# Last normalisation for all tokens beside the last expert unit, and that unit's own rows patched in behind it

## The chip, the cores and the metric

The kernel runs on one core of one Trainium2 chip. The metric is the device time of one execution in microseconds (us), the median of several. TensorE (PE) multiplies matrices, VectorE (DVE) and ScalarE (ACT) work elementwise, GpSimd (POOL) does small elementwise work and issues the indirect and the accumulating DMAs, SyncE (SP) issues plain DMAs.

## What is computed

The input is 8 x 512 = 4096 tokens of 256 floats. The first half of the reference (two attentions and a normalisation with a residual) isn't touched by the change. The second half is a mixture of experts with its own normalisation and residual:

```
logits = xf @ w_router;  probs = softmax(logits)
topk_w, topk_idx = top_k(probs, 2)            # each token: 2 of 8 experts
h   = gelu(einsum('te,ieh->tih', xf, w1) + b1)      # 256 -> 1024
out = einsum('tih,ihe->tie', h, w2) + b2            # 1024 -> 256
out = sum(out * weights, axis=1)
x = x + layernorm(ffn(layernorm(x)))
```

So a token's output row is its kept row x plus the normalised sum of two expert rows. A normalisation needs both.

## The kernel before

Stage 1 computes x (kept in the SBUF tile `X`, 32 rows of 256 in each of 128 partitions) and scatters every token's row twice into the HBM tensor `expert_rows`, sorted by expert. Tables made on VectorE (`fill_tables`) cut these rows into 39 subtiles of 256.

Stage 2 (`stage2`) runs 23 units over them: units 0 to 15 are pairs (two subtiles, 4 blocks of 128 rows), units 16 to 22 are singles (2 blocks). Unit t does this:

- SP loads the expert's weights into `WG1` and `WG2`; POOL gathers the unit's rows into `XG` (`gather_rows`, L1514), one indirect DMA for each block, two units ahead.
- TensorE turns the rows (`turn`, L1772), multiplies by the first weights into `PH` (`first`, L1761) and by the second ones into `PY` and `PB` (`second`, L1792 and L1793). ScalarE applies gelu (L1603) and makes the high parts of weights and hidden values, VectorE the low parts (L1691, L1696, L1702).
- VectorE computes the unit's gates `G` (`note`, L1681), POOL the weighted bias `BW` (`weigh_bias`, L1539), VectorE the result rows `Y` (`result`, L1659 and L1662), in the first groups of the next unit.
- POOL scatters `Y` with an add into the HBM tensor `choice_rows` (`send`, L1528), one indirect DMA for each block. `send(t)` waits until those of unit t-1 have landed, since both may hit the same row.

Every engine's order is fixed by the loops over t, over the groups j of the first product and over the eight chunks c of the second one: POOL gathers for t+2 and sends t-1 in the last group of t, and weighs the bias of t+1 at c = 6. Semaphores do the rest. While units 5 to 9 run, SP writes the kept rows of five of the eight batches to the output tensor `out` (L1492).

Stage 3 (`stage3`) starts when all of `choice_rows` has landed. SP loads it batch by batch (512 rows, `YC`, L1861). For each batch VectorE makes mean and variance (L1900 to L1906), POOL the inverse root (L1875, L1877), ScalarE the normalised rows `T` (L1914). The first five batches are then added by POOL to the kept rows in `out` with an accumulating DMA (L1881); for the last three VectorE adds `X` (L1894) and SP stores the sum (L1865).

## Time and profile before

| | us |
|---|---|
| median of 3 runs (1081.58 to 1086.25) | 1084.42 |
| the profiled execution, its own time | 1075.38 |
| its span, first to last instruction | 1073.6 |
| last matmul of the last unit starts | 1036.81 |
| first load of stage 3 is issued | 1043.30 |
| PE busy / DVE / ACT / POOL | 974.2 / 676.9 / 730.8 / 403.8 |
| mean granted TensorE clock | 0.968 |

The busy times are averages over stages with different limits. What is late at the end is read from the last 60 us, in which TensorE first works at nearly 100% and then not at all.

### The profile page before, as it was taken

To read this page: it belongs to the slowest core of one execution; us is meant where nothing else is said; L and a number is where in the kernel's file an instruction comes from. 1 tells how busy PE (TensorE), PEld (TensorE's weight loads), DVE (VectorE), ACT (ScalarE), POOL (GpSimd) and SP (SyncE) were. 2 spreads that over 40 slices of the span, in tenths; PEclk is the share of its full clock that TensorE was granted. 3 is DMA by queue.
4 is the path that set the end of the run, shared out by engine and by line. 5 is a ranking of instruction groups with operands and counts; after the bars stand their busy time and mean duration, and the time that the engine had idled before them with its cause. 6 is when DMAs were issued, how large, how long until landed. Compare 5 with 4: busy or idle time off the path is not lost.

```text
span 1073.6 us, 16809 instructions
## 1 busy us (share of the span) xinstructions
PE 974.2 (91%) x5468; PEld 659.2 (61%) x5468; DVE 676.9 (63%) x1882; ACT 730.8 (68%) x1124; POOL 403.8 (38%) x348
## 2 busy tenths in 40 slices
PE   5799999999999999978889988999999999998960
PEld 3233545455454545434588877888888888888850
DVE  5235286564838654554785789567766776777857
ACT  3688777777867777756737554676666677666836
POOL 4101020413223050304334357655555545545436
PEclk9899999999999999989999999999999999999995
DMA  7664726437181684822413443856655545567839
GB/s 277 140 231 85 263 46 213 126 102 251 39 270 56 227 300 114 320 82 90 158 61 104 104 128 69 262 154 152 157 158 135 171 128 119 123 166 215 235 56 287
DMA packets 57695, 171.12 MB, mean 159 GB/s; under 512 B 10384, under 2 KB 26896, under 8 KB 51728
## 3 DMA queue, kind: packets, MB, share of 16 engines
q1 hardware_dynamic: 38698, 137.99, 38.7%
q0 software_dynamic: 18768, 31.76, 15.5%
q8 instruction: 39, 0.64, 0.3%
q10 hardware_dynamic: 150, 0.41, 0.2%
q14 instruction: 40, 0.33, 0.1%
HBM read 98.55 MB, written 71.57 MB: 158 GB/s over the span
## 4 chain that ended last, share of the span: by engine, by line
PE 69%; DVE 13%; ACT 6%; issue 5%; DMA 3%; POOL 3%; ACTq 0%; SPq 0%; DVEq 0%; POOLq 0%
PE PH L1761 15%; PE PO L979 8%; PE PS L996 8%; PE PB L1059 7%; PE PY L1792 5%; PE PB L1792 4%; ACT E L603 3%; PE PY L1797 3%; PE PA L1046 3%; PE PY L1793 3%; PE PA L1027 3%; PE PB L1793 2%; DVE HP L1702 2%; PE PA L1036 1%; PE PT L1772 1%
## 5 line engine op out<-in xcount | busy, mean ns | idle before, releaser
L603 ACT ACTIVATE E<-PS,VV 128x1024 f32<-128x1024 f32 x256 | 271.2, 1118 | 66.9 <-PE PS L996 66.7
L1761 PE MATMUL PH<-XP,W1P 128*128 128x512 f32 (+1 forms) x1104 | 231.3, 367 | 13.5 <-DVE HP L1702 9.0
L1761 PEld LDWEIGHTS PH<-XP,W1P 128*128 128x128 f32 x1104 | 184.3, 191 | 54.7 <-DVE HP L1702 12.7
L1528 POOL DMA_INDIRECT choice_rows<-Y,DI x78 | 130.5, 1673 | 119.4 <-DVE Y L1662 96.8
L996 PE MATMUL PS<-OPB,OPA 102*128 102x512 bf16 x512 | 140.1, 388 | 13.4 <-ACT E L603 7.2
L1702 DVE TENSOR_TENSOR HP<-PH,HP 128x512 fp32r<-128x512 f32 x156 | 106.8, 686 | 65.5 <-ACT HP L1608 65.2
L979 PE MATMUL PO<-E,VA 128*32 128x512 f32 x1024 | 144.9, 616 | 0.0
L1603 ACT ACTIVATE PH<-PH,B 128x512 f32<-128x512 f32 (+1 forms) x184 | 107.5, 596 | 52.3 <-PE PH L1761 43.1
L996 PEld LDWEIGHTS PS<-OPB,OPA 102*128 102x128 bf16 x512 | 36.9, 98 | 160.1 <-ACT E L603 81.5
L1594 ACT CAST W2P<-WG 128x512 fp32r<-128x512 f32 x92 | 56.7, 621 | 102.2 <-PE PB L1793 63.2
L469 POOL DMA_INDIRECT expert_rows<-PAY,SLOT x64 | 63.0, 985 | 155.9 <-issue 81.9
L1792 PE MATMUL PY<-W2P,HP 128*128 128x512 f32 x288 | 108.5, 407 | 2.2 <-DVE Y L1662 2.2
L1696 DVE TENSOR_TENSOR W2P<-WG,W2P 128x512 fp32r<-128x512 f32 x92 | 74.6, 818 | 55.3 <-ACT W2P L1594 54.0
L1608 ACT CAST HP<-PH 128x512 fp32r<-128x512 f32 x156 | 91.6, 587 | 4.9
L1514 POOL DMA_INDIRECT XG<-expert_rows,RI x78 | 81.9, 1050 | 26.7 <-issue 22.7
L1793 PE MATMUL PY<-W2P,HP 128*128 128x256 f32 x288 | 80.5, 279 | 0.0
L1792 PE MATMUL PB<-W2P,HP 128*128 128x512 f32 x176 | 65.4, 395 | 0.0
L1691 DVE TENSOR_TENSOR W1P<-WG,W1P 128x512 fp32r<-128x512 f32 x92 | 59.7, 687 | 8.4 <-ACT W1P L1587 8.3
L1792 PEld LDWEIGHTS PY<-W2P,HP 128*128 128x128 f32 x288 | 54.1, 188 | 15.2 <-DVE Y L1662 3.8
L1797 PE MATMUL PY<-W2P,HP 128*128 128x256 f32 x480 | 63.1, 289 | 0.0
L1539 POOL TENSOR_TENSOR BW<-WG,G 128x1024 f32<-128x1024 f32 (+1 forms) x23 | 41.7, 1813 | 54.0 <-DVE G L1681 54.0
L491 POOL TENSOR_TENSOR SM<-SM,HALF 128x4 f32<-128x4 f32 x16 | 18.4, 1150 | 113.3 <-DVE SM L206 113.3
(244 smaller groups left out, 1559.4 us busy)
## 6 DMA issues: line engine op xcount, KB each, us to landing
expert_rows<-ZERO SPq DMA_DIRECT2D x8, 4160.0 KB, 12.9
WG<-experts SPq DMA_DIRECT2D x23, 1152.0 KB, 5.8
WG<-experts SPq DMA_DIRECT2D x23, 1028.0 KB, 5.2
OPB<-q_parts SPq DMA_DIRECT2D x192, 64.0 KB
q_parts<-QP SPq DMA_DIRECT2D x48, 128.0 KB
OPA<-q_parts SPq DMA_DIRECT2D x31, 192.0 KB
choice_rows<-ZERO SPq DMA_DIRECT2D x1, 5120.0 KB, 14.4
X<-x SPq DMA_DIRECT2D x8, 512.0 KB, 8.0
```

What stands on the lines that cost most here:

```text
L603: a.activation(E[:, s % 2, h, :, :], PS[:, u % 2, :, :], ACT.Exp, scale=vec("tau_t")[:, 4 * (s // 2) + h:4 * (s // 2) + h + 1]).then_inc(e ...
L979: i = t.matmul(PO[32 * h:32 * h + 32, :], VA[:, par, 2 * jp + jc, 4 * g + h, :], E[:, s % 2, h, jc, :], start=(jp == 0 and jc == 0), stop= ...
L996: ins = t.matmul(PS[:, u % 2, jc, :], OPA[0:KA, m, key:key + P], OPB[0:KA, m, hh * N:hh * N + N], start=True, stop=True)
L1514: g.indirect_dma_start(out=XG[:, t % 2, i, :], out_offset=None, in_=rows, in_offset=IND(ap=RI[:, b // HALVES, b % HALVES:b % HALVES + 1], ...
L1528: g.indirect_dma_start(out=ys, out_offset=IND(ap=DI[:, t % 3, i:i + 1], axis=0), in_=Y[:, t % 2, i, :], in_offset=None, compute_op=ALU.add ...
L1603: last = a.activation(r, r, ACT.Gelu_apprx_tanh, bias=B1[:, n * j + k:n * j + k + 1])
L1608: a.copy(region(0, j), PH[:, u % BANKS, :]).then_inc(h_hi, 1)
L1702: v.tensor_tensor(region(1, j), PH[:, u % BANKS, :], region(0, j).bitcast(f32), ALU.subtract).then_inc(h_lo, 1)
L1761: last = m.matmul(PH[:, u % BANKS, at:at + w], W1P[:, a, k * HID + c * P:k * HID + c * P + P], XP[:, o, k, 0:w], start=(k == 0 and (a, o) ...
L1792: m.matmul(sums(i), HP[:, 0, at:at + P], W2P[:, c, :, :], start=(c == 0), stop=(c == HC - 1), skip_group_check=True)
L1793: last = m.matmul(sums(i)[:, 0, :], HP[:, 1, at:at + P], W2P[:, c, 0, :], start=False, stop=(c == HC - 1), skip_group_check=True)
L1797: last = m.matmul(PY[:, i, :], HP[:, a, at:at + P], W2P[:, c, o, :], start=(c == 0 and (a, o) == terms[0] and i % 2 == 0), stop=(c == HC - ...
```

## The change

It moves three things.

1. One pair is put behind the singles: units 0 to 14 are pairs, 15 to 21 singles, and unit 22, the last, is a pair. Tables keep their layout (`entry_of`, `subtile_of`).
2. Stage 3 for all tokens runs beside unit 22. It waits for the sends of units 20 and 21 only, loads `choice_rows` into `X`, normalises in place and adds all eight batches into `out` with accumulating DMAs. So that `X` is free, SP writes all eight batches of kept rows beforehand, each twice: to `out` and to a new HBM tensor `kept_rows`. For the rows of unit 22 what it writes isn't final.
3. Unit 22 isn't sent to `choice_rows`. POOL gathers, by the token numbers `TO` of its 4 x 128 rows, their kept rows (`gather_kept`) and what the other units have summed for them (`gather_partial`). VectorE adds the latter to `BW`, so that `result` gives whole rows in `Y`; these are normalised like a batch, their kept rows added, and POOL scatters them over `out` (plain writes, `out_patched`), each of the four scatters waiting until the one before has landed, the first until all eight adds have.

One small comparison (`HOLDS`) is new in the tables: it sets the gates of unit 22 to zero if the unit holds no rows.

```diff
-KEPT = 5
...
+    xs = nc.dram_tensor("kept_rows", (TOK, D), f32, kind="Internal").ap()
...
+def is_pair(t):
+
+    return t < PAIRS - 1 or t == NUNITS - 1
+
+
+def entry_of(t):
+
+    return t if t < PAIRS - 1 else PAIRS - 1 if t == NUNITS - 1 else t + 1
...
-    return 2 * HALVES if t < PAIRS else HALVES
+    return 2 * HALVES if is_pair(t) else HALVES
...
-    return HID // P if t < PAIRS else HID // P // 2
+    return HID // P if is_pair(t) else HID // P // 2
...
-    return first_block(t) // HALVES
+    e = entry_of(t)
+    return 2 * e if e < PAIRS else PAIRS + e
...
+    link(v.tensor_tensor(HOLDS[:, :], first[:, 2 * LEFT_PAIRS - 2:2 * LEFT_PAIRS - 1], limit[:, 2 * LEFT_PAIRS - 2:2 * LEFT_PAIRS - 1], ALU.is_lt))
...
+    TBL = blocks_of(LAST)
+    kept, partial = (WG1[:, k * TB * D:(k + 1) * TB * D].rearrange("p (i e) -> p i e", e=D) for k in range(2))
...
+    PARTIAL = [(t, 16 * turn_blocks(t)) for t in (LAST - 1, LAST - 2)]
...
-            row = nc.sync.value_load(WI[0:1, t:t + 1], min_val=0, max_val=(NE - 1) * P)
+            row = nc.sync.value_load(WI[0:1, entry_of(t):entry_of(t) + 1], min_val=0, max_val=(NE - 1) * P)
...
-            if BEGUN <= t < BEGUN + KEPT:
+            if BEGUN <= t < BEGUN + B:
                 b = t - BEGUN
                 sp.wait_ge(begun["x1_added"], b + 1)
-                sp.dma_start(out[b * N:(b + 1) * N].rearrange("(p c) e -> p c e", c=C), X[:, C * b:C * b + C, :]).then_inc(begun["x_kept"], 16)
+                for place in (out, xs):
+                    sp.dma_start(place[b * N:(b + 1) * N].rearrange("(p c) e -> p c e", c=C), X[:, C * b:C * b + C, :]).then_inc(begun["x_kept"], 16)
+        sp.wait_ge(begun["x_kept"], 16 * 2 * B)
+        for t, sent in PARTIAL:
+            sp.wait_ge(y_sent[t % 2], sent)
+        for b in range(B):
+            sp.dma_start(X[:, C * b:C * b + C, :], yv[b]).then_inc(loaded[b], 16)
+        sp.wait_ge(out_added, 16 * B)
+        sp.wait_ge(out_patched, 16 * TBL)
...
-                b = first_block(t) + i
+                s, k = subtile_of(t) + i // HALVES, i % HALVES
                 g.indirect_dma_start(out=XG[:, t % 2, i, :], out_offset=None, in_=rows,
-                                     in_offset=IND(ap=RI[:, b // HALVES, b % HALVES:b % HALVES + 1], axis=0)
+                                     in_offset=IND(ap=RI[:, s, k:k + 1], axis=0)
...
-                if t == NUNITS - 1:
-                    pool.wait_ge(y_ready, first_block(t) + i + 1)
-                elif i == 0:
+                if i == 0:
                     pool.wait_ge(y_ready, first_block(t + 1))
...
+        def gather_kept():
+            pool.wait_ge(begun["x_kept"], 16 * 2 * B)
+            pool.wait_ge(g_ready, LAST + 1)
+            pool.wait_ge(w1_lo, PIECES * NUNITS)
+            pool.wait_ge(b1_ready, NUNITS)
+            for i in range(TBL):
+                g.indirect_dma_start(out=kept[:, i, :], out_offset=None, in_=xs, in_offset=IND(ap=TO[:, i:i + 1], axis=0)
+                                     ).then_inc(kept_back, 16)
+
+        def gather_partial():
+            for t, sent in PARTIAL:
+                pool.wait_ge(y_sent[t % 2], sent)
+            for i in range(TBL):
+                g.indirect_dma_start(out=partial[:, i, :], out_offset=None, in_=ys, in_offset=IND(ap=TO[:, i:i + 1], axis=0)
+                                     ).then_inc(partial_back, 16)
+
+        def root(n, var, nmean, r, bias):
+            pool.wait_ge(var_ready, 2 * n + 2)
+            g.tensor_tensor(r, var, half[:, 0:C], ALU.pow).then_inc(roots, 1)
+            pool.wait_ge(roots, n + 1)
+            g.tensor_tensor(bias, nmean, r, ALU.mult).then_inc(scaled, 1)
+
+        def add_out(b):
+            pool.wait_ge(normed, C * (b + 1))
+            g.dma_start(ov[b], X[:, C * b:C * b + C, :], accum_op=ALU.add).then_inc(out_added, 16)
+
+        def finish():
+            for b in range(B):
+                root(b, *(R[:, q, b, :] for q in range(4)))
+                if b >= 1:
+                    add_out(b - 1)
+            add_out(B - 1)
+            root(B, *(RL[:, q, :] for q in range(4)))
+            pool.wait_ge(out_added, 16 * B)
+            for i in range(TBL):
+                pool.wait_ge(rows_done, i + 1)
+                if i >= 1:
+                    pool.wait_ge(out_patched, 16 * i)
+                g.indirect_dma_start(out=out, out_offset=IND(ap=TO[:, i:i + 1], axis=0), in_=Y[:, LAST % 2, i, :], in_offset=None
+                                     ).then_inc(out_patched, 16)
...
-                    if j == groups_of(t) - 1:
+                    if j == groups_of(t) - 1 and t < LAST:
                         if t + 2 < NUNITS and t + 2 != BEGUN:
                             gather_rows(t + 2)
                         if t >= 1:
                             send(t - 1)
+                    if j == 1 and t == LAST:
+                        send(t - 1)
+                        gather_partial()
...
+                    if c == HC - 1 and t == LAST - 1:
+                        gather_kept()
...
-            send(NUNITS - 1)
+            finish()
...
+            for b in range(B):
+                act.wait_ge(scaled, b + 1)
+                for c in range(C):
+                    a.activation(X[:, C * b + c, :], X[:, C * b + c, :], ACT.Identity, scale=R[:, 2, b, c:c + 1],
+                                 bias=R[:, 3, b, c:c + 1]).then_inc(normed, 1)
+            act.wait_ge(scaled, B + 1)
+            for i in range(TBL):
+                a.activation(Y[:, LAST % 2, i, :], Y[:, LAST % 2, i, :], ACT.Identity, scale=RL[:, 2, i:i + 1],
+                             bias=RL[:, 3, i:i + 1]).then_inc(rows_normed, 1)
...
+                if t == LAST:
+                    dve.wait_ge(partial_in, 1)
...
             notes.did(v.tensor_tensor(less, w0, w1, ALU.subtract))
+            if t == LAST:
+                notes.did(v.tensor_copy(TO[:, 0:n], token))
             notes.did(v.tensor_tensor(place, token, valid, ALU.mult))
             notes.wait()
             notes.did(v.scalar_tensor_tensor(share, e0, FE[:, s:s + 1], less, ALU.is_equal, ALU.mult))
             notes.did(v.tensor_tensor(DI[:, t % 3, 0:n], place, dump, ALU.add))
             notes.wait()
+            if t == LAST:
+                notes.did(v.tensor_tensor(share, share, w1, ALU.add))
+                notes.wait()
+                v.tensor_scalar(G[:, r, 0:n], share, HOLDS[:, 0:1], None, ALU.mult).then_inc(g_ready, 1)
+                return
...
-            for i in range(blocks_of(NUNITS - 1)):
-                result(NUNITS - 1, i)
...
+            def end_stats(rows, st, mv, var, nmean):
+                for c, src in enumerate(rows):
+                    link(v.bn_stats(st[:, c, :], src))
+                dve.wait_ge(links, linked[0])
+                for c in range(len(rows)):
+                    link(v.bn_aggr(mv[:, c, :], st[:, c, :]))
+                dve.wait_ge(links, linked[0])
+                v.tensor_scalar_add(var, mv[:, :, 1], EPS).then_inc(var_ready, 1)
+                v.tensor_scalar_mul(nmean, mv[:, :, 0], -1.0).then_inc(var_ready, 1)
+
+            dve.wait_ge(b2_ready, NUNITS)
+            dve.wait_ge(w2_lo, PIECES * NUNITS)
+            for b in range(B):
+                dve.wait_ge(loaded[b], 16)
+                end_stats([X[:, C * b + c, :] for c in range(C)], ST[:, b, :, :], MV[:, b, :, :], R[:, 0, b, :], R[:, 1, b, :])
+                if b == PARTIAL_AT:
+                    dve.wait_ge(partial_back, 16 * TBL)
+                    v.tensor_tensor(BW[:, LAST % 2, :, :], BW[:, LAST % 2, :, :], partial, ALU.add).then_inc(partial_in, 1)
+            for i in range(TBL):
+                result(LAST, i)
+            dve.wait_ge(y_ready, first_block(LAST) + TBL)
+            end_stats([Y[:, LAST % 2, i, :] for i in range(TBL)], STL, MVL, RL[:, 0, :], RL[:, 1, :])
+            dve.wait_ge(kept_back, 16 * TBL)
+            for i in range(TBL):
+                dve.wait_ge(rows_normed, i + 1)
+                v.tensor_tensor(Y[:, LAST % 2, i, :], Y[:, LAST % 2, i, :], kept[:, i, :], ALU.add).then_inc(rows_done, 1)
...
-def stage3(nc, made, X, half, ys, out, y_sent, y_rows, x_kept):
```

POOL at the end of the program, before: the last two sends, then stage 3 with an add for each of five batches.

```order
L1539 TENSOR_TENSOR BW<-WG2,G 128x512
L1528 DMA choice_rows<-Y,DI 5120x256 x4
L1875 TENSOR_TENSOR RF<-RF,HALF 128x4
L1877 TENSOR_TENSOR RF<-RF 128x4
L1875 TENSOR_TENSOR RF<-RF,HALF 128x4
L1877 TENSOR_TENSOR RF<-RF 128x4
L1881 DMA out<-T 128x1024
```

POOL at the same place, after. WG1 and WG2 are the weight tiles, free by then, of which the new rows and statistics use parts.

```order
L1577 TENSOR_TENSOR BW<-WG2,G 128x1024
L1586 DMA WG1<-kept_rows,TO 128x256 x4
L1566 DMA choice_rows<-Y,DI 5120x256 x2
L1593 DMA WG1<-choice_rows,TO 128x256 x4
L1598 TENSOR_TENSOR WG2<-WG2,HALF 128x4
L1600 TENSOR_TENSOR WG2<-WG2 128x4
...
L1604 DMA out<-X 128x1024 x2
L1598 TENSOR_TENSOR WG2<-WG2,HALF 128x4
L1600 TENSOR_TENSOR WG2<-WG2 128x4
L1618 DMA out<-Y,TO 4096x256 x4
```

Four gathers now stand ahead of the last send and four behind it; the roots of all eight batches and their adds follow, and the four scatters of unit 22's rows stand last.

VectorE behind the last unit's hidden values, before: the last unit's results come first, then the statistics of the batches.

```order
L1702 TENSOR_TENSOR HP<-PH,HP 128x512 x2
L1659 SCALAR_TENSOR_TENSOR Y<-PY,G,BW 128x256
L1662 SCALAR_TENSOR_TENSOR Y<-PY,G,Y 128x256
...
L1900 BN_STATS STF<-YC 128x6 x4
L1903 BN_AGGR MVF<-STF 128x2 x4
```

VectorE after, from the fourth batch's statistics to the end.

```order
L1854 TENSOR_SCALAR WG<-WG 128x4
L1863 TENSOR_TENSOR BW<-BW,WG 128x1024
L1848 BN_STATS WG<-X 128x6 x4
...
L1754 SCALAR_TENSOR_TENSOR Y<-PB,G,BW 128x256
L1757 SCALAR_TENSOR_TENSOR Y<-PB,G,Y 128x256
L1848 BN_STATS WG<-Y 128x6 x4
L1851 BN_AGGR WG<-WG 128x2 x4
L1853 TENSOR_SCALAR WG<-WG 128x4
L1854 TENSOR_SCALAR WG<-WG 128x4
L1871 TENSOR_TENSOR Y<-Y,WG 128x256 x4
```

The statistics of all eight batches now stand ahead of the last unit's results, with the add of the partial rows among them.

## Rows read from the trace of the kernel before

**Rows 1.** Busy time by stretch: us, PE, PEld, DVE, ACT, POOL, clock, DMA, GB/s
```profile
1040.00:1073.00 33.00, 0.00 (x0) 0.00 (x0) 19.61 (x86) 16.37 (x32) 17.19 (x24) 0.52 0.93 262
```

**Rows 2.** The chain that ended last, from 1043: start us, us, what
```profile
1043.30 3.58 DMA YC<-choice_rows
...
1050.50 2.08 ACT T L1914 x4
...
1052.87 0.97 POOL out L1881
...
1062.26 0.91 POOL out L1881
...
1069.68 0.69 DVE T L1894
```

**Rows 3.** Timeline of PE: first products of units 15, 16, 21 and 22
```profile
922.04 11.40 PE L1761 MATMUL PH<-XP,W1P 128*128 128x512 f32 x48
944.92 5.77 PE L1761 MATMUL PH<-XP,W1P 128*128 128x256 f32 x48
1012.29 5.93 PE L1761 MATMUL PH<-XP,W1P 128*128 128x256 f32 x48
1024.77 5.87 PE L1761 MATMUL PH<-XP,W1P 128*128 128x256 f32 x48
```

**Rows 4.** Timeline: bias of a pair and of the last unit, unit 21's last result
```profile
918.86 1.89 POOL L1539 TENSOR_TENSOR BW<-WG,G 128x1024 f32<-128x1024 f32 x1 [2.67 <-DVE G L1681]
...
1025.47 1.42 POOL L1539 TENSOR_TENSOR BW<-WG,G 128x512 f32<-128x512 f32 x1 [2.65 <-DVE G L1681]
...
1030.63 0.48 DVE L1662 SCALAR_TENSOR_TENSOR Y<-PY,G,Y 128x256 f32<-128x256 f32 x1
```

**Rows 5.** Timeline of POOL: first and last of a pair's four gathers
```profile
874.46 1.29 POOL L1514 DMA_INDIRECT XG<-expert_rows,RI  x1 [0.15 <-issue]
...
878.61 0.96 POOL L1514 DMA_INDIRECT XG<-expert_rows,RI  x1 [0.30 <-issue]
```

**Rows 6.** Timeline of POOL: unit 21's second send, unit 22's first one
```profile
1033.72 1.57 POOL L1528 DMA_INDIRECT choice_rows<-Y,DI  x1 [0.30 <-issue]
...
1037.64 1.55 POOL L1528 DMA_INDIRECT choice_rows<-Y,DI  x1 [2.34 <-DMA choice_rows<-Y,DI]
```

**Rows 7.** Busy time by stretch, columns as in Rows 1: stage 3's loads, then adds
```profile
1043.30:1055.00 11.70, 0.00 (x0) 0.00 (x0) 7.83 (x41) 4.04 (x8) 4.51 (x6) 0.50 0.91 351
1055.00:1068.00 13.00, 0.00 (x0) 0.00 (x0) 9.55 (x44) 10.69 (x21) 11.63 (x17) 0.50 1.06 206
```

**Rows 8.** View of line L1881, the five accumulating DMAs: issue to landing
```profile
DMA to landing us min/median/max: 6.1/6.8/7.1
```

**Rows 9.** Timeline of POOL: a scatter, and what waited until it landed
```profile
651.31 1.37 POOL L469 DMA_INDIRECT expert_rows<-PAY,SLOT  x1 [0.31 <-issue]
655.01 1.59 POOL L1528 DMA_INDIRECT choice_rows<-Y,DI  x1 [2.33 <-DMA expert_rows<-PAY,SLOT]
```

**Rows 10.** Views of L1514 (gathers, all) and then L1528 (sends, from 1000)
```profile
DMA to landing us min/median/max: 2.7/3.9/8.1
...
DMA to landing us min/median/max: 3.6/3.7/4.4
```

**Rows 11.** Timeline of DVE: statistics of two batches in a row, and an add
```profile
1048.90 1.40 DVE L1900 BATCH_NORM_STATS2 STF<-YC 128x6 f32<-128x256 f32 x4
...
1050.89 1.40 DVE L1900 BATCH_NORM_STATS2 STF<-YC 128x6 f32<-128x256 f32 x4
...
1064.29 1.23 DVE L1894 TENSOR_TENSOR T<-T,X 128x1024 f32<-128x1024 f32 x1 [0.91 <-ACT T L1914]
```

**Rows 12.** Timeline of PE: three units' starts; a store is issued in the first
```profile
758.96 11.41 PE L1761 MATMUL PH<-XP,W1P 128*128 128x512 f32 x48
782.30 11.40 PE L1761 MATMUL PH<-XP,W1P 128*128 128x512 f32 x48
805.51 11.42 PE L1761 MATMUL PH<-XP,W1P 128*128 128x512 f32 x48
```

More of the change, by code:

```diff
@@ L191, in program @@
         FE = sb("FE", [P, SUBTILES], f32)
+        HOLDS = sb("HOLDS", [P, 1], f32)
         def const(name):
@@ L927, in vector_program @@
             do["begin"] = begin
-            sections = fill_tables(nc, dve, table_links, rows_known, tables_ready, COUNT, TAKEN, const,
+            sections = fill_tables(nc, dve, table_links, rows_known, tables_ready, COUNT, TAKEN, HOLDS, const,
                                    OT[:, :, :].rearrange("p g n -> p (g n)"), tables)
@@ L1165, in program @@
             inner = ExitStack()
-            y_sent, y_rows, experts = stage2(nc, make(inner), tables, tables_ready, const, rows, ys, experts1, experts2, begun, PB, X, out)
+            experts = stage2(nc, make(inner), tables, tables_ready, const, rows, ys, experts1, experts2, begun, PB, X, xs, HOLDS,
+                             HALF[:, :, :].rearrange("p a c -> p (a c)"), out)
             inner.close()
-            last = stage3(nc, make(apart), X, HALF[:, :, :].rearrange("p a c -> p (a c)"), ys, out, y_sent, y_rows, x_kept)
             block = apart.enter_context(nc.Block())
@@ L1174, in _ @@
                 experts.sync(sp)
-                last.sync(sp)
             @block.gpsimd
@@ L1182, in _ @@
                 units()
-                last.gpsimd(pool)
             @block.scalar
@@ L1190, in _ @@
                 units()
-                last.scalar(act)
             @block.vector
@@ L1198, in _ @@
                 units()
-                last.vector(dve)
             @block.tensor
@@ L1284, in fill_begun, with fill_tables @@
     dve.sem_inc(begun_ready, 1)
-def fill_tables(nc, dve, table_links, rows_known, tables_ready, COUNT, TAKEN, const, free, tables):
+def fill_tables(nc, dve, table_links, rows_known, tables_ready, COUNT, TAKEN, HOLDS, const, free, tables):
     v, ALU, AX = nc.vector, mybir.AluOpType, mybir.AxisListType
@@ L1386, with stage2 @@
 Experts = collections.namedtuple("Experts", "sync gpsimd scalar vector tensor")
-def stage2(nc, made, tables, tables_ready, const, rows, ys, experts1, experts2, begun, PB, X, out):
+def stage2(nc, made, tables, tables_ready, const, rows, ys, experts1, experts2, begun, PB, X, xs, HOLDS, half, out):
     f32, f32r, i32 = mybir.dt.float32, mybir.dt.float32r, mybir.dt.int32
@@ L1430, in stage2 @@
     NOTES = 4
+    LAST = NUNITS - 1
+    PARTIAL_AT = 3
+    TO = sb("TO", [P, TB], i32)
+    TBL = blocks_of(LAST)
+    kept, partial = (WG1[:, k * TB * D:(k + 1) * TB * D].rearrange("p (i e) -> p i e", e=D) for k in range(2))
+    ends, at = [], 0
+    for n in (B * C * 6, B * C * 2, 4 * B * C, TB * 6, TB * 2, 4 * TB):
+        ends.append(WG2[:, at:at + n])
+        at += n
+    ST, MV, R = (x.rearrange("p (b c k) -> p b c k", b=B, c=C) if k < 2 else x.rearrange("p (k b c) -> p k b c", b=B, c=C)
+                 for k, x in enumerate(ends[0:3]))
+    STL, MVL, RL = (x.rearrange("p (i k) -> p i k", i=TB) if k < 2 else x.rearrange("p (k i) -> p k i", i=TB)
+                    for k, x in enumerate(ends[3:6]))
+    loaded = [sem(f"y_loaded{b}") for b in range(B)]
+    var_ready, scaled, normed, roots = sem("var_ready"), sem("scaled"), sem("normed"), sem("roots")
+    out_added, links, out_patched = sem("out_added"), sem("finish_links"), sem("out_patched")
+    kept_back, partial_back, partial_in = sem("kept_back"), sem("partial_back"), sem("partial_in")
+    rows_normed, rows_done = sem("rows_normed"), sem("rows_done")
+    yv = ys[0:TOK].rearrange("(b p c) e -> b p c e", p=P, c=C)
+    ov = out.rearrange("(b p c) e -> b p c e", p=P, c=C)
     def turn_blocks(t):
         return sum(blocks_of(u) for u in range(t % 2, t + 1, 2))
+    PARTIAL = [(t, 16 * turn_blocks(t)) for t in (LAST - 1, LAST - 2)]
     def piece(tile, q):
@@ L1606, in hidden @@
             if t >= 1:
-                act.wait_ge(y_region, first_group(t - 1) + j + 1)
+                act.wait_ge(y_region, first_group(t - 1) + min(j, groups_of(t - 1) - 1) + 1)
             a.copy(region(0, j), PH[:, u % BANKS, :]).then_inc(h_hi, 1)
@@ L1737, in units, with link @@
                     at_slot(first_slot(t) + groups_of(t) + c)
-            for i in range(blocks_of(NUNITS - 1)):
-                result(NUNITS - 1, i)
+            linked = [0]
+            def link(i):
+                linked[0] += 1
+                i.then_inc(links, 1)
+            def end_stats(rows, st, mv, var, nmean):
[23 more added lines that the diff above has]
+                v.tensor_tensor(Y[:, LAST % 2, i, :], Y[:, LAST % 2, i, :], kept[:, i, :], ALU.add).then_inc(rows_done, 1)
         return units
@@ L1920, in constants @@
+    return Experts(sync, gpsimd, scalar, vector, tensor)
 def constants():
```

73 lines of the change are left out of this document (removed).

## The prediction

> **What bounds the kernel now.** I read three views. First the busy time by stretch: from 1040 to 1073 TensorE does nothing, while the DMA engines are 93% busy [rows 1]. So what the kernel can win here is cover for these last 30 us, and the currency is DMA time. Second the chain that ended last: the last unit's sends land, stage 3's first load is issued at 1043.30, the first add at 1052.87, the fifth at 1062.26, and VectorE's last add ends at 1070.4 [rows 2]; its store ends the span at 1073.6. Third the timeline of TensorE, for when units start: 922.04, 944.92, 1012.29, 1024.77 [rows 3]. Stage 3 therefore begins 18.5 us after unit 22 does and takes 30.3 us.
>
> **Part 1, the order of units.** The products are the same in number; one pair's period (944.92 - 922.04 = 22.9) leaves the stretch ahead of the last unit and one single's period (1024.77 - 1012.29 = 12.5) enters it. The change from pairs to singles, at which the first periods are longer, comes one unit earlier and costs the same. Units 16 to 21 took 1024.77 - 944.92 = 79.9; with one single more the seven, 15 to 21, take 92.3, and unit 22 starts at 922.04 + 92.3 = 1014.4 [rows 3]. Its rows are turned 512 wide instead of 256 and VectorE and ScalarE are in step with TensorE there: I add 0.4. The comparison HOLDS stands in a chain of dependent table steps; its price is less than the 0.48 of a 128x256 operation [rows 4], I take 0.2. Start: **1015.0** (1014.4 to 1017, should a pair's load or gather come late behind a single). TensorE ends at about 1015 + 22.9 = 1037.9, and nothing late waits for it any more: VectorE reaches unit 22's results only behind eight batches of statistics.
>
> **Part 2, when the loads may start.** They wait for the sends of unit 21. Its results are ready 1030.63 + 0.48 - 1024.77 = 6.3 after the last unit's start [rows 3, 4], at 1021.3. But POOL comes later. Its bias step began 0.7 after the unit's start, now 0.25 later for the extra small steps in the notes, and takes 1.89 instead of 1.42 [rows 4]: 1015.95 to 1017.85. Behind it stand the four gathers of kept rows, 0.15 + 5.1 (874.46 to 879.57 for a pair's four) [rows 5]: to 1023.1. Then two sends of 1.6: the first at 1023.4, the second 1.9 later at 1025.3, landing 3.7 behind its issue [rows 6, 10]: **1029.0**. The kept gathers so cost 1.8 us on the path, the one place where their issue isn't hidden. The loads go out at 1029.0, where before they went at 1043.30: 14.3 earlier.
>
> **Part 3, all tokens.** From the loads to the first add it was 1052.87 - 1043.30 = 9.6, and the adds followed one another by (1062.26 - 1052.87) / 4 = 2.35, POOL's own pace of root, bias and issue [rows 2]. POOL issues four more gathers (5.1) first, from 1029.3 to 1034.4, and the first variance is there at 1029.0 + 3.6 + 2.0 = 1034.6 [rows 2, 11]: hidden, with 0.2 to spare. So the adds go out at 1038.6, ... the seventh at 1052.7. The eighth has its root just before the seventh is issued and waits for 2.08 of ScalarE: 1054.8. What lands last is set by the engines: in the stretch of adds they are full and move 206 GB/s [rows 7], which is 0.524 MB / 206 = 2.55 us for a batch, more than POOL's 2.35. Eight of them are 20.4, where before five were adds and three were stores. From the loads' issue: 11.7 for the loads [rows 7], 1.5 for the 0.52 MB of partial rows at 351 GB/s, 20.4 for the adds: 1029.0 + 33.6 = 1062.6. The other way, 1054.8 + 7.1, the longest landing [rows 8], plus the growth of 0.2 us for each further add, gives 1062.3. I take **1062.4** (1060.9 with the shortest landing of 6.1; 1064.9 if an add costs 2.84, the 14.2 us from the loads' end to the fifth landing, divided by five).
>
> **Part 4, unit 22's own rows.** VectorE: statistics of a batch every 2.0, eight from 1032.6 to 1048.6; the partial rows' add 1.23 [rows 11]; four results of two operations, 4 x 1.0 [rows 4]; their statistics 2.0; so 1055.9. POOL's root, 1.3, to 1057.4; ScalarE 2.1, 1059.5; the last row add 1059.9. This is 2.5 us ahead of the adds' landing, which hides it all, the wait for the partial rows too as long as they land by 1043. Then the scatters, one after another. Their price the trace shows once: a plain scatter of 128 rows issued at 651.31 let the next instruction go at 655.01, **3.7 us** [rows 9]. Bounds: 3.0 from the fastest gather (2.7 + 0.3), 4.7 from the slowest late send (4.4 + 0.3) [rows 10]. I take 3.7, the row of the same kind. Four of them from 1062.7 land at 1062.7 + 14.8 - 0.3 = 1077.2. With the 0.4 that the end takes the span is **1077.6**, 4.0 more than before.
>
> A general fit weighs against this row. The Trainium skill (DMA: Bandwidth & Descriptors, Anatomy of one DMA) gives a DMA issued by POOL 2.0 us plus its bytes at 436 GB/s; for 128 KB that is 2.3, four steps of 2.6 with the next issue would be 10.4 instead of 14.8, and the span by it 1073.2. Rows 9 and 10 show no late indirect DMA that fast. Its rule against an accumulate beside another access of the same bytes (same page, Rules for kernel authors) is why all scatters stand behind all adds; by it none of the 14.8 us can be overlapped with the adds.
>
> **Part 5, the other additions.** Eleven more half-megabyte stores run beside units 5 to 12. A unit in which one is issued took 782.30 - 758.96 = 23.3, the next without one 805.51 - 782.30 = 23.2 [rows 12]. I take nothing; the cover is some 20 us of slack that a pair's loads have. Exposed, a store would be 1.5 us at 351 GB/s; I keep 1 us in all at the upper end.
>
> **Sum.** The last unit starts 9.8 earlier (1024.8 to 1015.0); the wait from there to the loads shrinks from 18.5 to 14.0; from the loads to the end it grows from 30.3 to 48.6 (33.4 to the last add, 14.8 scatters, 0.4). That is -9.8 - 4.5 + 18.3 = **+4.0 us**. The profiled execution had 1075.38, so 1079.4 for one like it. The three timed runs have their median 9.0 above that execution; the difference is carried over to it: 1084.42 + 4.0 = **1088.4**.
>
> **The rivals.**
> - *The patch costs more than the cover gives (slower by over 0.5%, which is 5.4 us and about what a measurement of this kernel can tell from no change).* The mechanism is the serial tail: four round trips behind the last add. It decides from a step of 4.05 us, or from adds of 2.73 us each. For it: the output rows are written in random order right behind 4 MB of adds, and sends did take 4.4. Against: nothing else moves then. Steps of 4.7 and adds of 2.84 give 1077.6 + 4.0 + 2.3 = 1083.9, 10.3 more: 1094.7.
> - *A cheap patch.* Steps of 3.0: 1074.8, and with the shortest landing of the adds 1073.3; a time of 1084 to 1086, no difference. For it: the fastest gather. The skill's fit lands here too.
> - *The adds don't bind, VectorE's chain does.* If 206 GB/s is only POOL's pace and the adds have landed when VectorE's last row add ends at 1059.9, the scatters start at 1060.2; with steps of 3.0 the end is 1072.3, 1.3 less than before. Faster by over 0.5%, that is an end under 1068.2, needs steps of 2.0 as well, which no row shows. Against it also stands the engines' share of 1.06 [rows 7].
> - *The change doesn't do what it says:* the loads wait for unit 22 after all. Only if POOL's sends of unit 21 were late by 14 us; nothing queued there is that long. 1 in 50, and then 1102.
>
> **Chances.** Forecast (within +1.5 to +5.4 us) 0.42; cheap patch (-5.4 to +1.5) 0.18; slower 0.35, with the last rival in it; faster by over 0.5% 0.05. The range goes from -2.4 to +10.6: 1082 to 1095. The likeliest case's own range is 1086 to 1090.
>
> **What would show it.** After: the first product of unit 22 near 1015; X's first load near 1029; eight adds 2.35 to 2.6 apart, the last landing near 1062; VectorE's last add ended before that; four scatters 3.7 apart; TensorE at work until 1038 and on no late part of the chain. I'm wrong if the scatters' step isn't 3.7, if POOL is held up between its gathers and the first root, or if the loads don't overlap with unit 22.

## The result, and the profile after

The changed kernel takes 1092.53 us (median of 7 runs, 1088.47 to 1094.04), the kernel before beside it 1083.76 (7 runs, 1081.05 to 1086.25): a ratio of 1.0075, interval 1.0057 to 1.0092, or 8.1 us more (6.2 to 10.0). The forecast was 4.0 more, 1088.4, with a range of 1082 to 1095. The time lies in the range, but not in the likeliest case (1.5 to 5.4 us more, 0.42): it falls to the rival that was given 0.35, slower by over 0.5%. One execution of the last kernel below, two_stored, took 3361.7 us, for a reason that nothing here shows, and is left out of its ratio.

The profiled execution has a span of 1086.6 us. Its timeline of PE, at the first products of units 15, 21 and 22 (start us, us, engine, line, operation, what ended the idle time ahead), answers to [rows 3]:

```profile
927.23 0.98 PE L1893 MATMUL PH<-XP,W1P 128*128 128x256 f32 x7
...
1008.20 0.98 PE L1893 MATMUL PH<-XP,W1P 128*128 128x256 f32 x6 [0.94 <-DVE XP L1787]
...
1021.13 1.19 PE L1893 MATMUL PH<-XP,W1P 128*128 128x512 f32 x4 [0.27 <-DVE XP L1787]
```

SyncE issues the loads of `X` here, 14.6 behind unit 22's start:

```profile
1035.73 4.02 SPq L1530 DMA_DIRECT2D X<-choice_rows  x8
```

Then the timeline of POOL: the bias step of unit 22, the first kept gather, the two sends of unit 21 [rows 4 to 6], the first partial gather, the first, second and eighth add [rows 2], and the four scatters:

```profile
1022.17 2.26 POOL L1577 TENSOR_TENSOR BW<-WG,G 128x1024 f32<-128x1024 f32 x1 [3.25 <-DVE G L1781]
1024.59 1.29 POOL L1586 DMA_INDIRECT WG<-kept_rows,TO  x1 [0.15 <-issue]
...
1029.97 1.62 POOL L1566 DMA_INDIRECT choice_rows<-Y,DI  x1 [0.30 <-issue]
1031.90 1.57 POOL L1566 DMA_INDIRECT choice_rows<-Y,DI  x1 [0.30 <-issue]
1035.94 1.02 POOL L1593 DMA_INDIRECT WG<-choice_rows,TO  x1 [2.47 <-DMA choice_rows<-Y,DI]
...
1045.35 1.00 POOL L1604 DMA_DIRECT2D out<-X  x1 [0.46 <-ACT X L1727]
...
1048.64 0.94 POOL L1604 DMA_DIRECT2D out<-X  x1
...
1062.67 0.85 POOL L1604 DMA_DIRECT2D out<-X  x1 [1.36 <-ACT X L1727]
...
1070.67 1.12 POOL L1618 DMA_INDIRECT out<-Y,TO  x1 [5.81 <-DMA out<-X]
1074.03 1.01 POOL L1618 DMA_INDIRECT out<-Y,TO  x1 [2.24 <-DMA out<-Y,TO]
1077.26 0.97 POOL L1618 DMA_INDIRECT out<-Y,TO  x1 [2.21 <-DMA out<-Y,TO]
1080.44 0.97 POOL L1618 DMA_INDIRECT out<-Y,TO  x1 [2.21 <-DMA out<-Y,TO]
```

VectorE's four row sums, which the scatters wait for as well, end at 1067.4:

```profile
1065.60 1.83 DVE L1871 TENSOR_TENSOR Y<-Y,WG 128x256 f32<-128x256 f32 x4 [3.17 <-ACT Y L1731]
```

The busy time by stretch (columns as in [rows 1]) shows the two parts of the tail that are new, a stretch of accumulates that fill the DMA engines, and one in which nearly nothing runs:

```profile
1050.00:1070.00 20.00, 0.00 (x0) 0.00 (x0) 13.64 (x58) 13.24 (x26) 12.55 (x18) 0.50 1.04 205
...
1073.00:1087.00 14.00, 0.00 (x0) 0.00 (x0) 0.00 (x0) 0.00 (x0) 2.95 (x3) 0.50 0.08 28
```

The views of the lines 1604 (adds) and 1618 (scatters) give the time from issue to landing, and SyncE's waits from 1040 on give what stands at the end (engine and line, what it waited for, total us, times, longest):

```profile
DMA to landing us min/median/max: 6.8/7.3/7.7
...
DMA to landing us min/median/max: 2.4/2.4/2.6
...
SPq L1532 <- DMA out<-Y,TO: 43.1, 1, 43.1
SPq L1166 <- PEq L1166: 3.4, 1, 3.4
```

The last scatter lands at about 1080.44 + 2.5 = 1082.9, and 3.7 us pass from there to the end. SyncE spends 3.4 of them in the last wait that its queue shows, at line 1166, which I read as the closing barrier of the block. In the kernel before, that wait is 0.2 us, and the forecast had 0.4 for the whole end:

```profile
SPq L1164 <- PEq L1164: 0.2, 1, 0.2
```

The profiled span is 13.0 us longer than that of before, the medians differ by 8 to 9. So part of the 13.0 is chance of single executions, and the first experiment asks which part.

### The profile page after: what moved, and what is told of

Its sections match the earlier page's. It is cut to its first block, busy times and chain, and to the rows that moved or that the text cites. A ratio compares the mean times of both kernels' runs of the same rounds, so it can differ in the third digit from the quotient of the medians.

```text
span 1086.6 us, 16855 instructions
## 1 busy us (share of the span) xinstructions
PE 977.9 (90%) x5468; PEld 660.8 (61%) x5468; DVE 680.3 (63%) x1894; ACT 732.7 (67%) x1128; POOL 411.9 (38%) x359
## 4 chain that ended last, share of the span: by engine, by line
PE 65%; DVE 14%; ACT 7%; issue 5%; DMA 3%; POOL 2%; another core or an unknown queue 2%; ACTq 0%; POOLq 0%; SPq 0%; DVEq 0%
PE PH L1893 15%; PE PO L981 8%; PE PS L998 8%; PE PB L1061 6%; PE PY L1924 4%; ACT E L605 4%; PE PB L1924 3%; PE PY L1929 3%; PE PA L1029 3%; PE PA L1048 2%; PE PY L1925 2%; PE PB L1925 2%; DVE HP L1804 1%; DVE W1P L1793 1%
## 5 line engine op out<-in xcount | busy, mean ns | idle before, releaser
L1893 PE MATMUL PH<-XP,W1P 128*128 128x512 f32 (+1 forms) x1104 | 233.9, 370 | 12.9 <-DVE HP L1804 7.1
L1566 POOL DMA_INDIRECT choice_rows<-Y,DI x74 | 123.5, 1668 | 103.9 <-DVE Y L1757 83.9
L1798 DVE TENSOR_TENSOR W2P<-WG,W2P 128x512 fp32r<-128x512 f32 x92 | 76.0, 835 | 52.4 <-ACT W2P L1678 51.2
L1924 PEld LDWEIGHTS PY<-W2P,HP 128*128 128x128 f32 x288 | 54.1, 188 | 14.6 <-DVE Y L1757 2.8
## 6 DMA issues: line engine op xcount, KB each, us to landing
choice_rows<-ZERO SPq DMA_DIRECT2D x1, 5120.0 KB, 14.6
```

The costliest lines, as they stand in the source:

```text
L1566: g.indirect_dma_start(out=ys, out_offset=IND(ap=DI[:, t % 3, i:i + 1], axis=0), in_=Y[:, t % 2, i, :], in_offset=None, compute_op=ALU.add ...
L1893: last = m.matmul(PH[:, u % BANKS, at:at + w], W1P[:, a, k * HID + c * P:k * HID + c * P + P], XP[:, o, k, 0:w], start=(k == 0 and (a, o) ...
L1924: m.matmul(sums(i), HP[:, 0, at:at + P], W2P[:, c, :, :], start=(c == 0), stop=(c == HC - 1), skip_group_check=True)
```

## The experiments

There are ten runs, eight of new kernels and two repeats, in three groups, each group on one chip beside the kernel before. The worth of a kernel is its ratio; where a ratio is given in us, it is taken of 1083.76. Of the traces I use stretches that begin at an event, not absolute times. The first product of unit 0 lies between 596.8 and 609.5 in the traces, and even on one chip at 596.8 (two_stored) and 601.6 (stores_only), though the changed kernel does nothing new ahead of it.

**a_again and b_again: the changed kernel and the kernel before once more, no edit.**

> The changed kernel again, with a profile. Between the two profiled executions the changed one lay 5.2 us behind already when unit 15 started (927.2 against 922.0), a place that nothing but one table comparison touches. Theory A (that part is chance between executions): here unit 15 starts anywhere from 922 to 928, while the times from unit 15's start to the end repeat within 1 us (159.4), and the ratio to the kernel before is 1.006 to 1.009. Theory B (the comparison or the code's other place costs it): unit 15 starts near 927 again, while the kernel before again shows 922. Either way the last 3.4 us, from the last scatter's landing to the end, should repeat if they belong to the kernel.

> The kernel before again, for a second profile of it. Theory A: unit 15 starts at 924 to 928 here, since the three timed runs had a median 9 us above the first profiled execution. Theory B: 922 again. From unit 15's start to the end 151.6 us, within 1 us, by both; from the last store's landing to the end 0.4.

The changed kernel came out at a ratio of 1.0078 (1.005 to 1.0106). Timeline of PE, first of a_again (units 15 and 22), then of b_again (the same):

```profile
922.17 1.10 PE L1893 MATMUL PH<-XP,W1P 128*128 128x256 f32 x8
...
1020.32 0.97 PE L1893 MATMUL PH<-XP,W1P 128*128 128x512 f32 x3 [0.27 <-DVE XP L1787]
```

```profile
921.81 1.55 PE L1761 MATMUL PH<-XP,W1P 128*128 128x512 f32 x6
...
1027.45 0.73 PE L1761 MATMUL PH<-XP,W1P 128*128 128x256 f32 x4 [0.58 <-DVE XP L1685]
```

On one chip both kernels reach unit 15 within 0.4 us. The 5.2 us that the changed kernel was late there in the first pair of traces were therefore chance; 4.5 of them were there at the first product of unit 0 already (603.8 against 599.3). Two expectations failed: the kernel before reached unit 15 at 921.8 and not at 924 to 928, and the time from unit 15 to the end did not repeat within 1 us (163.7 where 159.4 was expected, 155.7 where 151.6 was). From unit 15 to unit 22 the changed kernel took 98.2 here and 93.9 in the first trace; the kernel before 105.6 here and 102.7 in the first. The trace that the forecast was made from was the shortest of all that I have of that order in this stretch. From unit 22 to the end the changed kernel took 65.6 here and 65.5 in the first; the kernel before took 50.1 and 48.8.

**stores_only: the kernel before with the changed kernel's eleven further stores.**

```diff
-            if BEGUN <= t < BEGUN + KEPT:
+            if BEGUN <= t < BEGUN + B:
...
+                for place, kept in ((out if b < KEPT else spare, begun["x_kept"] if b < KEPT else extra), (xs, extra)):
+                    sp.dma_start(place[b * N:(b + 1) * N].rearrange("(p c) e -> p c e", c=C), X[:, C * b:C * b + C, :]).then_inc(kept, 16)
```

> The kernel before, with the changed kernel's eleven further half-megabyte stores alone: beside units 5 to 12 every batch of kept rows is written a second time to a spare table, and batches 5 to 7 a further time; nothing reads them. Theory A (part 5 of the prediction: the stores are hidden by the slack of the pairs' loads): unit 13 starts as in the kernel before within 1 us, the ratio is 1.000 within 0.001. Theory B (part of the changed kernel's 5 us over the forecast at unit 15 came from these stores): each holds up a weight load by up to 1.5 us beside a unit that has no slack; unit 13 starts 2 to 5 us later and the ratio is 1.002 to 1.005.

The ratio was 1.0002 (0.9979 to 1.0024). Timeline of PE, units 5 and 15, between which all the stores lie:

```profile
691.60 1.09 PE L1766 MATMUL PH<-XP,W1P 128*128 128x512 f32 x4
...
924.26 1.08 PE L1766 MATMUL PH<-XP,W1P 128*128 128x512 f32 x4
```

These are 232.7 us. The kernel before took 232.8 in its trace and 232.7 in b_again, the changed kernel 231.9 and 232.1. The stores cost nothing that these runs can tell.

**no_patch: the changed kernel without the four scatters.**

```diff
         sp.wait_ge(out_added, 16 * B)
-        sp.wait_ge(out_patched, 16 * TBL)
...
-            pool.wait_ge(out_added, 16 * B)
-            for i in range(TBL):
-                pool.wait_ge(rows_done, i + 1)
-                if i >= 1:
-                    pool.wait_ge(out_patched, 16 * i)
-                g.indirect_dma_start(out=out, out_offset=IND(ap=TO[:, i:i + 1], axis=0), in_=Y[:, LAST % 2, i, :], in_offset=None
-                                     ).then_inc(out_patched, 16)
+            pool.wait_ge(rows_done, TBL)
```

> Leaves out the four scatters of the last unit's rows over the output, so those 512 rows lack the last unit's part; all else stays. The trace of the changed kernel has 12.5 us from the eighth add's landing (1070.4) to the last scatter's, then 3.7 to the end. Theory A (the end's 3.4 us belong to POOL, whose last DMA is issued only 2.5 us before it lands, so that what POOL does to leave the program comes behind it): without scatters POOL is done 6 us before the last add lands, the end comes 0.4 behind that landing, and the time falls by 12.5 + 3.3 = 15.8 us, to about 7.5 us below the kernel before (ratio 0.993). Theory B (the end's wait has nothing to do with POOL): it falls by 12.5 alone, ratio 0.996.

The ratio was 0.9931 (0.9911 to 0.9951), 0.0146 below the changed kernel (1.0077, the middle of its two), which is 15.8 us. That is the value of theory A, the four steps and the end together, 12.5 + 3.3. But the intervals of the ratios leave some 3 us to each side, down to 13, which hardly parts it from the 12.5 of theory B, and the trace agrees with theory A only in part. The last add was issued at 1053.55 and landed, at most 9.1 behind, by 1062.65; the span ended at 1064.3, and that is 1.65 for the end and not 0.4. SyncE's waits, and the last piece of the chain that ended last:

```profile
SPq L1166 <- DMA out<-X: 32.3, 1, 32.3
SPq L1166 <- PEq L1166: 1.4, 1, 1.4
...
1057.89 0.42 DVE Y L1864
```

From unit 22 to the end it is 52.4, which is 13.1 less than in the changed kernel: 12.5 for the scatters and 2.0 for the end, less 1.5 because the adds landed later behind the loads (36.2 against 34.7). The chain does not run over the adds here but over VectorE's last row sum (1058.3), which only POOL waits for in this kernel. So the end may be POOL's here too, 6.0 behind its last wait; what fills these 6.0 us stays open, since in order_only, where POOL's last instruction ends 5.9 ahead of the end, SyncE's last wait is 0.2 again.

Without the patch the cover is a gain of 7.5 us by the ratio. The loss lies in what the patch adds: the scatters and the later end.

**patch_at_once: no wait of one scatter for the one before.**

```diff
                 pool.wait_ge(rows_done, i + 1)
-                if i >= 1:
-                    pool.wait_ge(out_patched, 16 * i)
                 g.indirect_dma_start(out=out, out_offset=IND(ap=TO[:, i:i + 1], axis=0), in_=Y[:, LAST % 2, i, :], in_offset=None
```

> The four scatters one after another without waiting for the one before: their rows are different. In the changed kernel they were issued 3.36, 3.23 and 3.18 apart, and an indirect DMA that waits for nothing follows another after 1.27. If the step is the round trip, as the prediction has it, three steps of 3.26 become three of 1.3: 5.9 us less than the changed kernel, ratio to the kernel before 1.002. If instead their transfers, in random order over 4 MB, are what takes the time, they queue up and less than 2 us is won.

The ratio was 1.0008 (0.9988 to 1.0028). Timeline of POOL:

```profile
1066.39 1.12 POOL L1616 DMA_INDIRECT out<-Y,TO  x1 [6.46 <-DMA out<-X]
1067.81 1.01 POOL L1616 DMA_INDIRECT out<-Y,TO  x1 [0.30 <-issue]
1069.13 0.97 POOL L1616 DMA_INDIRECT out<-Y,TO  x1 [0.30 <-issue]
1070.41 0.97 POOL L1616 DMA_INDIRECT out<-Y,TO  x1 [0.31 <-issue]
```

The step is 1.34 instead of 3.26, and each scatter still lands 2.4 behind its issue. From unit 22 to the end it is 60.4 instead of 65.5, 5.1 less; by the ratios it is 7.5 less, and both are near the 5.9 worked out ahead. The waits between the scatters, which they don't need (their rows are distinct; only the entries that fill up a block repeat a row, with the same values), were over a third of the patch. The end stays: the last one lands at 1072.9, the span ends at 1076.3.

**pool_last: the kernel before, with one tiny POOL instruction behind the last store.**

```diff
+        pool.wait_ge(stored, 16 * (len(CHUNKS) - BY_STORE))
+        g.memset(END[:, :], 0.0)
```

> The kernel before, with POOL kept in the program to the end: it waits until the last stores have landed and then writes 128 single floats; no DMA of its own is added. Theory A (what POOL does to leave the program costs some 3 to 5 us behind its last instruction; in the kernel before POOL was done early and this was hidden): the end comes 3 to 5 us later, ratio 1.003 to 1.005, and the engines' last wait in the trace grows from 0.2 to over 3. Theory B (the 3.4 us belong to the indirect DMAs that POOL issued shortly before): under 0.5 us, ratio 1.000.

The ratio was 1.0028 (1.0007 to 1.0048), 3.0 us more for a 0.1 us instruction. POOL's timeline and SyncE's wait:

```profile
1089.62 0.10 POOL L1884 MEMSET END<- 128x1 f32 x1 [6.77 <-DMA out<-T]
...
SPq L1164 <- PEq L1164: 3.9, 1, 3.9
```

The span ended at 1093.7, 4.0 behind the end of that instruction, and from unit 22 to the end it took 53.7 where the kernel before has 49.9 as a mean of three. So with POOL last, and with no DMA of its own in flight, the end comes some 4 us behind what it does. In the trace of before POOL's last instruction ends at 1067.42, 6.2 ahead of the span's end, which would hide this; in the changed one POOL issues the last scatter at 1080.44, and the end shows. I tried no kernel in which another engine is the last, so whether this is POOL's own or one of any engine whose last work is late is open; SyncE's wait of 0.2 in the kernel before, where its own wait for the last store ended last, shows only that SyncE doesn't pay it.

**adds_plain: the eight accumulating DMAs as plain copies.**

```diff
-            g.dma_start(ov[b], X[:, C * b:C * b + C, :], accum_op=ALU.add).then_inc(out_added, 16)
+            g.dma_start(ov[b], X[:, C * b:C * b + C, :]).then_inc(out_added, 16)
```

> The changed kernel with its eight adds issued as plain copies, so that the output lacks the kept rows of the tokens outside the last unit. Theory A (an accumulating DMA takes the engines twice the work of a copy, 2.55 us for 0.52 MB, and eight of them bind): with copies the engines are idle between them, each lands within 4 us of its issue instead of 7.2, and the end falls by 3.5 to 4.5 us: ratio 1.004 against 1.0078. Theory B (POOL's pace of 2.35 binds and 7 us is the latency of a direct DMA that POOL issues): landing stays near 7, nothing is won.

The ratio was 1.002 (0.9999 to 1.004), 6 us less than the changed kernel's, where 3.5 to 4.5 had been expected; from unit 22 to the end it is 4.8 less. The landing of the copies, the first scatter, and the busy time from 1050 to 1070, the same stretch as above:

```profile
DMA to landing us min/median/max: 2.9/3.1/6.5
...
1069.81 1.09 POOL L1618 DMA_INDIRECT out<-Y,TO  x1 [1.98 <-DVE Y L1871]
...
1050.00:1070.00 20.00, 0.00 (x0) 0.00 (x0) 17.14 (x72) 15.54 (x31) 13.56 (x22) 0.55 0.68 274
```

At 205 GB/s the engines are full with accumulates (share 1.04), at 274 GB/s with copies they are not (0.68). Per MB that is 1.04 / 205 against 0.68 / 274, twice as much. (The second stretch holds the end of the loads as well; from 1055 to 1066, where only copies run, it is 0.65 at 265 GB/s, the same per MB.) Now VectorE's row sums release the first scatter, 30.2 us behind the first load (1039.60); in the changed kernel it was the adds' landing, 34.9 behind it (1035.73). That is the 4.7 by which the adds bound the tail.

**order_only: the kernel before with its last unit a pair, behind the singles; nothing else moved but the indices and one wait of ScalarE that follow from it.**

```diff
+def is_pair(t):
+    return t < PAIRS - 1 or t == NUNITS - 1
...
-    return 2 * HALVES if t < PAIRS else HALVES
+    return 2 * HALVES if is_pair(t) else HALVES
```

> The kernel before with the order of units of the changed one: a pair behind the singles, and nothing else; its last stage still waits for the last unit. By the prediction the last unit ends where it ended, 0.6 us later, and then four sends instead of two stand between it and the last stage: 2 x 1.9 us more, less what the per-block order hides: 3 to 5 us slower, ratio 1.003 to 1.005. A rival (a pair's gathers behind a single hold up the weights' load, as TensorE's 0.9 us of idle time at unit 21 in the changed kernel hints) adds 1 to 2 us: 1.006.

The ratio was 1.0012 (0.9994 to 1.003), 1.3 us more, less than expected. From unit 22 to the end it took 1085.9 - 1026.0 = 59.9, where the kernel before took 48.8, 50.1 (b_again) and 50.8 (stores_only). So a larger last unit that nothing covers costs 10 us in the tail, and its earlier start gives back 8.7 of them. This is the other side of the trade: the new order alone brings nothing.

**patch_split: patch_at_once, and two of the four kept gathers behind the sends.**

```diff
                         send(t - 1)
+                        gather_kept(range(TBL // 2, TBL))
                         gather_partial()
...
-                        gather_kept()
+                        gather_kept(range(TBL // 2))
```

> The four scatters at once, and two of the four gathers of kept rows moved from ahead of the last send to behind it, where POOL sat idle 2.5 us until the send had landed. In the changed kernel the last unit's bias step ended at +3.3 us from the unit's start, the four gathers at +8.5, the first send went at +8.8, though the results that it sends are ready at +6.3. Theory A (POOL's issue is on the path there): the first send goes at +6.4, the loads 2.4 us earlier than in the changed kernel (+12.2 instead of +14.6), the end 2.4 us earlier than with the four scatters at once alone: ratio to the kernel before 0.998 to 0.999. Theory B (the loads gain nothing that reaches the end, since the adds are paced elsewhere): 1.001.

The ratio was 0.9998 (0.9979 to 1.0018), 0.0010 below patch_at_once, where 2.4 us had been expected. Timeline of POOL, the bias step, the sends, and the later kept gathers, and then the landing of the loads on line 1530 (6.3/9.4/11.8 in the changed kernel):

```profile
1031.55 2.26 POOL L1577 TENSOR_TENSOR BW<-WG,G 128x1024 f32<-128x1024 f32 x1 [3.25 <-DVE G L1780]
...
1038.15 1.62 POOL L1566 DMA_INDIRECT choice_rows<-Y,DI  x1 [1.61 <-DVE Y L1756]
1040.08 1.57 POOL L1566 DMA_INDIRECT choice_rows<-Y,DI  x1 [0.30 <-issue]
1041.95 1.02 POOL L1586 DMA_INDIRECT WG<-kept_rows,TO  x1 [0.30 <-issue]
...
DMA to landing us min/median/max: 8.2/10.6/13.6
```

Two things took the gain. The send now waits for VectorE's result (DVE Y), which is ready 6.9 behind the unit's start and not 6.3, and POOL issues 0.8 later still, so the loads come 12.4 behind the bias step instead of 13.6: 1.2 less, not 2.4. And six gathers now run beside the loads, which land later; that the one is the reason of the other isn't shown. The bias step to the first add is 22.9 us against 23.2.

**two_stored: patch_split, and the last two batches summed on VectorE and stored, not accumulated.**

```diff
+    late = XG[:, :, :, 0:D]
...
+            if b == BY_ADD:
+                sp.wait_ge(xt_full, KC * NUNITS)
+                sp.wait_ge(g_ready, NUNITS)
+            sp.dma_start(batch(b), yv[b]).then_inc(loaded[b], 16)
+        for b in range(BY_ADD, B):
+            sp.wait_ge(summed, b - BY_ADD + 1)
+            sp.dma_start(ov[b], batch(b)).then_inc(stored, 16)
...
+                v.tensor_tensor(batch(b), batch(b), X[:, C * b:C * b + C, :], ALU.add).then_inc(summed, 1)
```

> The kernel patch_split (the changed kernel with the kept rows fetched in two halves and no wait between the scatters), with one more edit: the last two batches of choice rows are loaded into the memory of the gathered rows, which nothing reads any more; VectorE adds the kept rows to them there, and SyncE writes them to the output by two plain stores, in place of two accumulating DMAs; their two stores of kept rows into the output early on fall away. Theory A (the DMA engines, at 2.55 us for an accumulated batch and about 1.3 for a copied one, decide when the scatters may start): two of the eight cost 1.25 us less each, so first load to first scatter shrinks from patch_split's 36.0 us (1043.95 to 1079.9) by 2.5 us to about 33.5, and VectorE's row adds, 3 us ahead of the last landing in patch_split, are then only just ahead; the ratio falls by 0.0023 to about 0.9975. Theory B (the queue's fixed times decide, the last store being issued later than the last add was): VectorE's sums end 2.5 us behind the last normed batch, the stores are issued about where the last two adds were, and nothing is gained: 36 us, ratio 0.9998 as patch_split.

The ratio was 0.9977 (0.9956 to 0.9997), the value of theory A; it is the one kernel here with all its work done whose interval lies below 1, by a hair. SyncE's timeline, first loads and the two stores, and POOL's first scatter:

```profile
1024.36 3.04 SPq L1541 DMA_DIRECT2D X<-choice_rows  x6
...
1052.29 1.71 SPq L1544 DMA_DIRECT2D out<-XG  x2
...
1058.48 1.11 POOL L1630 DMA_INDIRECT out<-Y,TO  x1 [5.03 <-DMA out<-XG]
```

Loads to first scatter is 34.1, not 36.0 as in patch_split: 1.9 of the 2.5. The rest went where theory B had it: the scatter waits for the stores (out<-XG), which are issued 5.6 behind the last of six adds (1046.71), because VectorE takes the sums up only behind the statistics of unit 22's rows.

## Why the prediction was right or wrong

- **Part 1, the order.** Forecast 9.8 earlier. The traces give 93.9 us on average from unit 15 to 22 in eight traces of the new order (90.8 to 98.2) and 105.2 in four of the old (102.7, 105.6, 106.3, 106.0), 11.3 less. The other way round, what each ratio leaves when the tail's difference (unit 22 to end, less 49.9, the mean of three) is taken off:

| kernel | tail us | tail less 49.9 | ratio's us | left to the order |
|---|---|---|---|---|
| changed, first | 65.5 | +15.6 | +8.1 | -7.5 |
| changed, a_again | 65.6 | +15.7 | +8.4 | -7.3 |
| no_patch | 52.4 | +2.5 | -7.5 | -10.0 |
| patch_at_once | 60.4 | +10.5 | +0.9 | -9.6 |
| patch_split | 59.6 | +9.7 | -0.2 | -9.9 |
| adds_plain | 60.7 | +10.8 | +2.2 | -8.6 |
| order_only | 59.9 | +10.0 | +1.3 | -8.7 |
| two_stored | 57.0 | +7.1 | -2.5 | -9.6 |

The mean is -8.9. The term was right within its uncertainty, but a part of that was luck: the profile of before was its quickest in that stretch, by 3 us, and the new order's stretch, forecast at 93.0, varies by 7 us between executions.
- **Part 2, the loads.** Forecast 14.0 behind unit 22's start, measured 14.6. The mechanism (four kept gathers ahead of the sends) was there. The bias step took 2.26, not 1.89, and began 1.04 behind the start instead of 0.95. patch_split shows that the gathers cost the path 1.2, not 1.8: with two of them gone VectorE's result is what the send waits for, and the 1.8 left out the 0.8 us from that result to POOL's issue.
- **Part 3, all tokens.** Forecast 33.4 from loads to last landing, measured 34.65. The adds follow one another by (1062.67 - 1045.35) / 7 = 2.47, and only one gap, the first, is large (3.29); the rest are 2.34 on average, 2.35 as read. Landing was 7.7 at the worst, not 7.1. (The forecast's second way to the last landing adds up to 1062.5, not 1062.3, with 0.2 for each of three further adds; it took 1062.4 and nothing hangs on it.) That the engines bound this part and not POOL's pace was right: adds_plain.
- **Part 4, the patch.** VectorE's sums ended at 1067.4, 3.0 ahead of the adds' landing (2.5 forecast). The step was 3.26, not 3.7, 2.3 less to the last landing than by the forecast. In [rows 9] the 3.7 are 1.37 of issue and 2.33 of waiting; the scatters here are issued in 0.97 to 1.01 and waited for 2.2 more. The difference is nearly all in the issue: the scatter of [rows 9] was the last of a series of eight, and in the changed kernel's trace the last of that series takes 1.32 as well, the others about 1.0:

```profile
654.58 0.97 POOL L471 DMA_INDIRECT expert_rows<-PAY,SLOT  x1 [0.30 <-issue]
655.86 1.32 POOL L471 DMA_INDIRECT expert_rows<-PAY,SLOT  x1 [0.30 <-issue]
```

By the general fit of the Trainium skill (DMA: Bandwidth & Descriptors, Anatomy of one DMA) I estimate 2.3 us for these bytes, and the measured landing of 2.4 agrees; the step is longer than the fit by the 0.8 us between a landing and the next issue, which I had put at 0.3.
- **The end.** This is the step that failed: "With the 0.4 that the end takes". It took 3.7 behind the last landing. The 0.4 was read from a program in which a DMA of SyncE is the last work, and was carried to one in which POOL's is. pool_last shows it: one small POOL instruction behind the last landing moves the end to 4.0 behind it. no_patch fits by its ratio; in its trace only 2.0 of the 3.3 went, so it is no second proof.
- **Part 5, the stores.** Nothing, as forecast: stores_only.
- **Sum.** Of the terms behind unit 22's start, +0.6, +1.25, -2.3 and +3.3 make 2.85 more than forecast; the kernel before's own tail is 49.9 as a mean and not 48.8, which takes 1.1 back. So 4.0 + 1.75 = 5.8 by the tail, and 0.9 less of the order makes 6.7, inside the interval of 6.2 to 10.0. What is over that, 1.4 to 1.7 us in the two measurements of the changed kernel, I can't place; their intervals are 2 and 3 us wide to each side. That the time lies in the range is thus partly the work of errors that cancel, -2.3 in the scatters against +3.3 at the end.

Of the rivals the one with a serial tail (0.35 with the last) had the sign and the place, but not the mechanism: neither a step above 4.05 nor an add above 2.73 made it slower. Steps were cheaper than forecast, and the program's end took back more than they gave. The rival in which VectorE's chain binds is what adds_plain is; by that run the changed kernel was 4.7 us away from it.

## What to carry to other kernels

Price the last few microseconds of a program by who does the last thing: a tail that ends with a DMA of POOL isn't the tail of one that ends with a DMA of SyncE, and the end of the old profile doesn't hold for the new. A chain of dependent small scatters costs a round trip each, so first ask whether the waits between them are needed, and count an accumulated byte as two copied ones when DMA engines are what a stage is short of. When a forecast is a difference of two long stretches, take more than one execution of the kernel before: here one stretch of the same program varied by 3 us, as much as the effect looked for.

## What the runs showed of the hardware

- With POOL last, the span ends 4 to 5 us behind its work: 4.0 behind a memset of 0.1 us (pool_last), 5.2 and 4.9 behind the end of the last scatter's issue (changed kernel, patch_at_once), 3.7 and 3.4 behind that scatter's landing. SyncE's last wait is 3.9, 3.4 and 3.1 there, and 0.2 in the kernel before.
- An accumulating DMA from SBUF to HBM takes twice the engine time of a copy for the same bytes: share 1.04 at 205 GB/s against 0.68 at 274 GB/s, landing 6.8 to 7.7 us against a median of 3.1 (changed kernel, adds_plain).
- An indirect scatter of 128 rows of 1 KB into a quiet memory lands 2.4 us behind its issue, whether the others wait or follow every 1.3 us. Dependent ones follow every 3.26 (changed kernel), as POOL issues the next 0.8 behind a landing. Its issue takes POOL 0.97 to 1.12 us, that of an accumulating one 1.57 to 1.62.
- The same singles, in the same order, took 90.8 to 98.2 us for seven in different executions, five of them (90.8, 92.1, 93.9, 94.7, 98.2) with nothing changed up to that point.
